# Causal attention block: the maximum's mask moved from TensorE matmuls to VectorE, and the shift rows from TensorE and ScalarE to VectorE and DRAM

## What is computed

```python
def reference(x, w_in, w_out, W_r, W_k, W_v, mu_r, mu_k):   # x: 2 x 2048 x 256
    xn = layernorm(x)
    q, k, v = heads(xn @ w_in.T)                  # 16 heads of 16
    att = q @ k.T / 4
    att = where(tril, att, 0.0)                   # masked scores are 0, not minus infinity
    a = softmax(att) @ v
    r = sigmoid((mu_r*xn + (1-mu_r)*x_prev) @ W_r.T)
    kk = square(relu((mu_k*xn + (1-mu_k)*x_prev) @ W_k.T))
    return x + merge(a) @ w_out.T + r * (kk @ W_v.T)
```

## Time and profile before

| | us |
|---|---|
| median of 3 runs | 1128.43 |
| lowest, highest | 1125.78, 1129.91 |
| the profiled execution | 1134.35 |
| its span | 1132.6 |
| TensorE busy in the span | 1080.0 (95%) |
| VectorE busy | 842.5 (74%) |
| ScalarE busy | 713.4 (63%) |
| GpSimd busy | 385.8 (34%) |

### The profile page before, as it was taken

How to read it: one execution, slowest core, us unless ns; L and a number is a source line. 1 busy time by engine, 2 the same in 40 slices (tenths; PEclk the granted TensorE clock), 3 DMA queues, 4 the chain that set the end, 5 groups by cost and what they waited for, 6 DMA issues and landing times.

```text
span 1132.6 us, 21906 instructions
## 1 busy us (share of the span) xinstructions
PE 1080.0 (95%) x8192; PEld 542.6 (48%) x8192; DVE 842.5 (74%) x1153; ACT 713.4 (63%) x1519; POOL 385.8 (34%) x945
## 2 busy tenths in 40 slices
PE   5999998999999999999989999999999989999998
PEld 3665554544444444444435444444444434444445
DVE  5567787678879787987867878878887878789213
ACT  2433333267776677777757776777777657767672
POOL 3211121354414341444224424442532433244301
PEclk9999999999999899999969999999999989999999
DMA  3585744392019000900280019002800460002033
GB/s 127 174 271 177 214 149 149 131 117 62 2 20 122 30 3 17 124 31 7 37 119 11 6 22 140 8 7 38 124 6 6 58 104 7 6 2 86 25 98 117
DMA packets 53390, 83.61 MB, mean 74 GB/s; under 512 B 6308, under 2 KB 36260, under 8 KB 49572
## 3 DMA queue, kind: packets, MB, share of 16 engines
q1 hardware_dynamic: 52132, 78.01, 32.9%
q0 software_dynamic: 1152, 4.19, 1.2%
HBM read 43.78 MB, written 33.55 MB: 68 GB/s over the span
## 4 chain that ended last, share of the span: by engine, by line
PE 75%; DVE 13%; ACT 4%; issue 4%; DMA 2%; POOL 0%; SPq 0%; ACTq 0%; DVEq 0%; POOLq 0%
PE ps_o L1189 22%; PE ps_s L1175 21%; DVE part_max L347 10%; PE ps_m L330 7%; PE ps_vr L733 4%; ACT probs L1039 4%; PE ps_qk L724 4%; PE ps_m L1220 3%; PE ps_o L1200 2%; PE ps_m L337 2%; PE ps_xt L782 2%; PE ps_qk L733 2%; PE ps_s L1164 2%; DMA x_in<-x 1%; PE ps_pieces L330 1%
## 5 line engine op out<-in xcount | busy, mean ns | idle before, releaser
L1039 ACT ACTIVATE probs<-ps_s 128x512 f32<-128x512 f32 (+3 forms) x1280 | 599.6, 536 | 249.6 <-PE ps_s L1175 241.5
L347 DVE TENSOR_REDUCE part_max<-ps_m 128x2 f32<-128x1024 f32 (+2 forms) x594 | 616.6, 1059 | 152.7 <-PE ps_m L330 115.1
L1175 PE MATMUL ps_s<-q_op,k_op 50*128 50x512 f32 (+3 forms) x1280 | 447.9, 429 | 10.0 <-ACT probs L1039 5.2
L330 PE MATMUL ps_m<-k_op,q_op 48*128 48x512 f32 (+3 forms) x1188 | 355.3, 419 | 16.6 <-DVE part_max L347 9.4
L1175 PEld LDWEIGHTS ps_s<-q_op,k_op 50*128 50x128 f32 x1280 | 210.7, 188 | 313.1 <-ACT probs L1039 214.2
L984 POOL TENSOR_SCALAR_AFFINE_SELECT probs<-probs 128x128 f32<-128x128 f32 x512 | 145.0, 292 | 485.7 <-ACT probs L1039 477.2
L1189 PE MATMUL ps_o<-probs,v_sb 128*32 128x512 f32 (+3 forms) x2560 | 307.9, 551 | 2.2 <-issue 2.2
L330 PEld LDWEIGHTS ps_m<-k_op,q_op 48*128 48x128 f32 x1188 | 169.3, 189 | 43.8 <-DVE part_max L347 33.8
L950 POOL TENSOR_TENSOR diag_weight<-ident,masked_weight 128x256 f32<-128x256 f32 x256 | 150.5, 623 | 40.7 <-ACT masked_weight L1005 40.7
L337 PE MATMUL ps_m<-mask,pick 64*128 64x64 bf16 (+1 forms) x932 | 96.5, 210 | 0.0
L1189 PEld LDWEIGHTS ps_o<-probs,v_sb 128*32 128x32 f32 x2560 | 51.1, 108 | 76.7 <-issue 38.1
(11 more groups left out here) (81 smaller groups left out, 715.9 us busy)
## 6 DMA issues: line engine op xcount, KB each, us to landing
parts_d<-parts SPq DMA_DIRECT2D x32, 512.0 KB, 4.7
q_op<-parts_d SPq DMA_DIRECT2D x42, 256.0 KB, 13.9
k_op<-parts_d SPq DMA_DIRECT2D x42, 256.0 KB, 16.2
vpad_d<-v_pad SPq DMA_DIRECT2D x32, 256.0 KB, 3.3
v_sb<-vpad_d SPq DMA_DIRECT2D x8, 1024.0 KB, 12.4
x_in<-x SPq DMA_DIRECT2D x8, 512.0 KB, 5.2
ffn_d<-ffn SPq DMA_DIRECT2D x8, 512.0 KB, 3.2
attn_t<-normed SPq DMA_DIRECT2D x128, 32.0 KB, 2.0
```

Of the source, the lines that this page charges most:

```text
L330: last = pe.matmul(ps_m[:, f % ring * 2 + e, 0:width], self.q_op[rows, p, j, q0:q0 + P], self.k_op[rows, p, j, pc * CH:pc * CH + width], s ...
L347: dve.tensor_reduce(both, ps_m[:, bank:bank + 2, 0:width], AX_X, ALU.max).then_inc(self.piece_reduced, 1)
L1039: act.activation(probs[:, slot % PRING, 0:width], ps_s[:, bank_of("scores", slot, first, last), 0:width], ACT.Exp).then_inc(probs_ready, 1)
L1175: pe.matmul(ps_s[:, bank_of("scores", slot, first, last), 0:CH - q0], k_op[rows, p, h % 2, kt * P:(kt + 1) * P], q_op[rows, p, h % 2, u * ...
```

## The change

**TensorE** no longer adds the mask: the four L337 matmuls of each diagonal piece are gone (1024 in all), and so are the 32 turns of shift rows, four transposes each. **ScalarE** no longer copies them. The ring of `ps_s` banks has one use less for each.

**VectorE** reduces a diagonal piece in parts: the blocks left of the diagonal block as before, with one reduction (none where there is no such block), and the diagonal block of each head with one `tensor_tensor_reduce`, which adds the fp32 `mask` and takes the maximum in one pass, writes the sum back to PSUM and the maximum to `part_max`. It is built as two instructions, the pass and one that writes the maximum out. A fourth `max_step` transposes the 32 columns of `shift` in blocks of 32 x 32 into `shift_t`.

**SyncE** gets the shift rows from `shift_t` into `q_op` in two hops: four DMAs to a DRAM buffer `shift_d`, a wait until they have landed, four DMAs to `q_op`. And in `group`, the loads of the next group's queries and keys now stand behind `keep_normed` of the previous group's unit 3 and behind `place_shift` of unit 2.

```diff
@@ -211,12 +210,12 @@
         self.v_after = sb("v_after", [P, 2, NT, GH * HW])
         self.keys_after = sb("keys_after", [P, P])
         self.ones = sb("ones", [P, P])
-        self.mask16 = sb("mask16", [P, 2, P], BF16)
-        self.pick16 = sb("pick16", [P, 2, P], BF16)
+        self.mask = sb("mask", [P, P])
         self.part_max = sb("part_max", [P, NCH, GH * SUB, NCH + 1])
+        self.floor = sb("floor", [P, 2])
         self.row_max = sb("row_max", [P, NCH, GH, SUB])
         self.shift = sb("shift", [P, NCH, SUB, SHIFT_PARTS, GH])
-        self.shift_t = sb("shift_t", [SHIFT_PARTS * GH, 2, CH])
+        self.shift_t = sb("shift_t", [P, 2, HW])
 
         self.consts_set, self.consts_made = sem("consts_set"), sem("consts_made")
         self.q_loaded = [sem("q_loaded0"), sem("q_loaded1")]
...
@@ -229,36 +228,28 @@
         self.after_ready = sem("after_ready")
         self.ones_placed = sem("ones_placed")
         self.chunk_loaded = [sem(f"chunk_loaded{c}") for c in range(NCH)]
-        self.shift_turned, self.shift_t_ready = sem("shift_turned"), sem("shift_t_ready")
+        self.shift_t_ready, self.shift_stored = sem("shift_t_ready"), sem("shift_stored")
         self.shift_loaded = [sem("shift_loaded0"), sem("shift_loaded1")]
         self.SHIFTS = SHIFT_PARTS * 2 * 16
+        self.shift_d = nc.dram_tensor("shift_d", [2, SHIFT_PARTS, 2, GH // 2, CH], F32, kind="Internal").ap()
         self.parts_in = parts_d.rearrange("r (z b) (cc g e j d) t -> r z (b cc) g e d j t", b=B, cc=CC, g=2, e=2, j=GH // 2)
...
-        pool.memset(self.pick16[:], 0.0).then_inc(self.consts_set, 1)
+        pool.memset(self.mask[:], 0.0).then_inc(self.consts_set, 1)
+        pool.memset(self.floor[:], 0.0).then_inc(self.consts_set, 1)
         pool.memset(self.part_max[:], 0.0).then_inc(self.consts_set, 1)
         pool.memset(self.after[:, NT - 1], 0.0).then_inc(self.consts_set, 1)
         pool.wait_ge(self.consts_set, 5)
...
-                pool.wait_ge(self.consts_made, 1 + 4 * e + 2 * half)
-                mask, pick = self.mask16[rows, half], self.pick16[rows, half]
-                pool.affine_select(out=mask, in_=mask, compare_op=ALU.is_ge, fill=NEG, base=half * HALF,
-                                   pattern=[[-1, P]], channel_multiplier=1).then_inc(self.consts_made, 1)
-                pool.wait_ge(self.consts_made, 2 + 4 * e + 2 * half)
-                pool.affine_select(out=pick, in_=pick, compare_op=ALU.not_equal, fill=1.0, base=half * HALF,
-                                   pattern=[[-1, P]], channel_multiplier=1).then_inc(self.consts_made, 1)
-        pool.wait_ge(self.consts_made, 9)
-        floor = self.part_max[:, NCH - 1].rearrange("p (h s) c -> p h s c", s=SUB)[:, :, SUB - 1, NCH]
-        pool.affine_select(out=floor, in_=floor, compare_op=ALU.not_equal, fill=LOWEST,
-                           base=-(P - 1), pattern=[[0, GH]], channel_multiplier=1).then_inc(self.consts_made, 1)
+        pool.affine_select(out=self.mask[:], in_=self.mask[:], compare_op=ALU.is_ge, fill=NEG, base=0,
+                           pattern=[[-1, P]], channel_multiplier=1).then_inc(self.consts_made, 1)
+        pool.wait_ge(self.consts_made, 2)
+        pool.affine_select(out=self.floor[:], in_=self.floor[:], compare_op=ALU.not_equal, fill=LOWEST,
+                           base=-(P - 1), pattern=[[0, 2]], channel_multiplier=1).then_inc(self.consts_made, 1)
 
         for half in range(2):
             counts = self.v_after[:, half].rearrange("p t (h w) -> p t h w", w=HW)[:, :, :, HD:HW]
@@ -300,11 +291,16 @@
     def place_shift(self, sp, p, u, n):
 
         sp.wait_ge(self.shift_t_ready, n + 1)
+        sp.wait_ge(self.shift_loaded[u % 2], (n // 2 + 1) * self.SHIFTS)
+        by_block = self.shift_d[u % 2].rearrange("r e j (s b w) -> b s (r e j) w", s=SUB, w=HW)
+        for b in range(P // HW):
+            sp.dma_start(by_block[b], self.shift_t[b * HW:(b + 1) * HW, u % 2]).then_inc(self.shift_stored, 16)
+        sp.wait_ge(self.shift_stored, (n + 1) * (P // HW) * 16)
         for part in range(SHIFT_PARTS):
             for e in range(2):
-                row, at = e * HALF + ROWS + part, part * GH + e * 2
+                row = e * HALF + ROWS + part
                 sp.dma_start(self.q_op[row:row + 1, p, :, u * CH:(u + 1) * CH].bitcast(F32),
-                             self.shift_t[at:at + 2, u % 2]).then_inc(self.shift_loaded[u % 2], 16)
+                             self.shift_d[u % 2, part, e].unsqueeze(0)).then_inc(self.shift_loaded[u % 2], 16)
 
     def load_values(self, sp, i, p):
 
@@ -328,14 +324,7 @@
         for e in (1, 0):
             rows = slice(e * HALF, e * HALF + ROWS)
             last = pe.matmul(ps_m[:, f % ring * 2 + e, 0:width], self.q_op[rows, p, j, q0:q0 + P],
-                             self.k_op[rows, p, j, pc * CH:pc * CH + width], start=True, stop=(pc < u))
-        if pc == u:
-
-            for k in range(2):
-                for e in (1, 0):
-                    half = slice(e * HALF, (e + 1) * HALF)
-                    last = pe.matmul(ps_m[:, f % ring * 2 + e, s * P + k * HALF:width], self.pick16[half, k],
-                                     self.mask16[half, k, k * HALF:P], start=False, stop=(k == 1))
+                             self.k_op[rows, p, j, pc * CH:pc * CH + width], start=True, stop=True)
         last.then_inc(self.piece_ready, 1)
 
     def reduce_piece(self, dve, ps_m, ring, f, base):
@@ -343,8 +332,17 @@
         u, j, s, pc, width = piece(f)
         dve.wait_ge(self.piece_ready, base + f + 1)
         bank = f % ring * 2
-        both = self.part_max[:, u].rearrange("p (e j s) c -> p e j s c", j=GH // 2, s=SUB)[:, :, j, s, pc]
-        dve.tensor_reduce(both, ps_m[:, bank:bank + 2, 0:width], AX_X, ALU.max).then_inc(self.piece_reduced, 1)
+        by_pair = self.part_max[:, u].rearrange("p (e j s) c -> p e j s c", j=GH // 2, s=SUB)[:, :, j, s]
+        if pc < u:
+            dve.tensor_reduce(by_pair[:, :, pc], ps_m[:, bank:bank + 2, 0:width], AX_X, ALU.max).then_inc(self.piece_reduced, 1)
+            return
+        if s > 0:
+            dve.tensor_reduce(by_pair[:, :, pc], ps_m[:, bank:bank + 2, 0:s * P], AX_X, ALU.max)
+        for e in range(2):
+            block = ps_m[:, bank + e, s * P:width]
+            floor = self.floor[:, 0:1] if u == NCH - 1 and s == SUB - 1 else 0.0
+            last = dve.tensor_tensor_reduce(block, block, self.mask[:], 1.0, floor, ALU.add, ALU.max, by_pair[:, e, pc + 1:pc + 2])
+        last.then_inc(self.piece_reduced, 1)
 
     def max_step(self, dve, k, u, n, reduced):
 
@@ -361,6 +359,11 @@
             dve.wait_ge(self.hi_ready, n + 1)
             dve.scalar_tensor_tensor(by_head[1], self.row_max[:, u], -1.0, by_head[0], ALU.mult,
                                      ALU.subtract).then_inc(self.shift_ready, 1)
+        if k == 3:
+            dve.wait_ge(self.shift_ready, n + 1)
+            if n >= 2:
+                dve.wait_ge(self.shift_stored, (n - 1) * (P // HW) * 16)
+            dve.transpose(self.shift_t[:, u % 2], self.shift[:, u].rearrange("p s r h -> p (s r h)")).then_inc(self.shift_t_ready, 1)
 
     def after_piece(self, dve, f, n0, base, close):
 
...
@@ -889,16 +867,14 @@
                 sp.dma_start(out_tiles[n], total[n % ORING]).then_inc(out_stored[n % ORING], 16)
 
             def group(i, p, first=False, last=False):
-                if not last:
-
-                    if not first:
-                        sp.wait_ge(scores_ready, (i * 2 + p) * SLOTS)
-                    ops.load_scores(sp, i + p, 1 - p)
                 if not first:
                     keep_normed(i - 1 + p, 1 - p, NCH - 1)
                 ops.place_shift(sp, p, 2, unit_of(i, p, 2))
                 if not last:
 
+                    if not first:
+                        sp.wait_ge(scores_ready, (i * 2 + p) * SLOTS)
+                    ops.load_scores(sp, i + p, 1 - p)
                     sp.wait_ge(masked_done, unit_of(i, p, 0) + 1)
                     sp.wait_ge(probs_used, weighed_to(unit_of(i, p, 0)))
                     ops.load_values(sp, i + p, 1 - p)
...
-                    v = SHIFT_AT[u, kt]
-                    wait_for_bank("shift", v, i, p, first, last)
-                    turn_shift(v, unit_of(i, p, v + nxt), bank_of("shift", v, first, last))
+                    sum_suffix(1 - p, SV_AT[u, kt], G + 1, bank_of("suffix", SV_AT[u, kt], i * 2 + p))
 
             def group(i, p, first=False, last=False):
                 G = i * 2 + p
```

78 lines of the change are left out of this document (18 added, 60 removed).

## The result

The changed kernel takes **1181.6 us** (median of four runs, 1170.2 to 1199.9) where the kernel before takes 1129.2 beside it. The longest of the four counts as a slow run; without it the median is 1177.8 and the ratio 1.043, 95% interval 1.034 to 1.052. The kernel is slower, as forecast, and some 23 us less slow than forecast. The profiled execution is that longest one, 1199.9 us with a span of 1198.0.

A forecast was written before the change was run, and what follows sets the result against it. The prediction took a loop of TensorE and ScalarE waiting for each other, 2.67 us a key tile, as the bound, VectorE second. Terms 0 - 16 + 11 + 73.5 + 18 - 10 = +76.5 gave 1205 us against the median; range 1165 to 1240.

The forecast's parts named there:

- masks and passes: Diagonal pieces: mask matmuls off TensorE gain 0, being hidden; VectorE's added passes cost +11 us, +1.5 a group.
- turns of shift rows: Turns off TensorE and ScalarE: 32 tiles with a turn each become 0.5 us shorter, -16 us.
- losses of before: Waits for "issue" and low-clock slices near group starts, 19 us together; half taken as gone, -10 us.
- stops for late loads: Piece 0 of the next group waits for queries and keys: 12 us in six groups, 1.5 in the first.
- clock behind them: After each 12 us stop, some 9 us of work at the lower clock: 3 us, six times, +18.
- the choice inside the bounds: Wait of piece 0 for late loads, bounded at 9.8 to 15.7 us; 12 was taken.
- The row of the prediction for the price: Fourth group's 98 matmuls at half clock, 20.5 us against 13.4: 0.35 us lost per microsecond at the lower level.
- the rival with 20 us behind each stop: Clock stays low for 20 us after each stop: +7 six times in place of +3, 1229 us; chance 0.12.
- The rival of the full price: On VectorE, pass and second instruction do not overlap: +38 in place of +11, 1232 us; chance 0.10.
- the rival of TensorE as the bound: Mask matmuls count on TensorE, 0.26 us off each of 256 pieces: 1127 us with loads still late; chance 0.03.
- One rule for all tiles from rows 3: Key tiles last 2.67 us with or without mask matmuls, so masks cost nothing; at most 1 us a group.
- the hop "costs nothing": Shift rows' way through DRAM, some 4 us longer, is covered by many key tiles before a unit's first score.

The follow-up runs named there:

- 1096.2: Kernel before with shift rows through VectorE and DRAM, masks still on TensorE, SyncE issuing shift rows, then loads, then results: 1096.2 us, ratio 0.967.
- 1093.6: Changed kernel with SyncE issuing shift rows, then loads, then results, plus 128 met waits at the start of TensorE's program: 1093.6 us, ratio 0.966.
- 1108.6: Kernel before with only the masks moved to VectorE, plus 128 met waits at the start of TensorE's program: 1108.6 us, ratio 0.979.
- 1132.1: Kernel before, unchanged, timed beside one of the three sets of experiment kernels: 1132.1 us.
- 1094.1: Changed kernel with SyncE issuing unit 2's shift rows first, then query and key loads, then the previous group's results: 1094.1 us, ratio 0.966.

## Why the prediction was right, and what of it was wrong

The side, the deciding term and its place were right; the size was too high by 23 us. Its sum by parts, with what the runs show in place of each (differences of medians; the stops from the profiled execution):

| term | forecast | measured | from |
|---|---|---|---|
| masks and passes | 0 + 11 | -2.6 | 1096.2 (masks on TensorE) to 1093.6, within the noise |
| turns of shift rows | -16 | -15.0 | 1108.6 to 1093.6, no gap in either |
| losses of before | -10 | -20.8 | 1132.1 to 1096.2, less the turns |
| stops for late loads | +73.5 | +56.0 | the row of the waits |
| clock behind them | +18 | +31.5 | what is left: 1181.6 less 1094.1 less 56.0 |
| sum | +76.5 | +49.1 | |

Three terms were too high, the loads by 17.5 us, masks and passes by 13.6 and the losses of before by 10.8, and the clock's was too low by 13.5. The clock's row is a remainder, so the sum has to come out near the measured difference (1.043 is 49 us) and proves nothing; the rows for themselves count.

**Loads.** The working held to a microsecond: first load 23.9 us into the group forecast (475.0 less 451.1), 23.6 measured (the stores landed in 1.1 us, not in the 2.0 of a result); from first issue to last landing 30.2 to 36, measured 30.6; a stop of 9.8 to 15.7, measured 9.3 in the mean. The step that failed is the choice inside the bounds. I took 12 "nearer to the case that a row shows", to leave room for values that share the engines. They hardly do: the run with the values held back gained 0.9 us. The low end was the right one, 56 us in place of 72. The first group, for which I gave 1.5, had no stop.

**Clock.** Here the term was too small. I took 9 us at the lower level behind each stop. In the profiled execution each of the six stretches begins within its stop, which costs nothing yet, and goes on behind it, from the matmul of piece 0, for 31.5, 7.5, 33.2, 15.7, 41.8 and 4.6 us, 22 in the mean; a seventh, of 13.7 us in the last group, follows no stop. The row of the prediction for the price was good: in the second group nearly the same work, from piece 0 on, takes 30.8 us in the change and 20.7 us with the loads in time:

```profile
383.70:414.50 30.80, 30.80 (x139) 13.54 (x143) 18.14 (x67) 14.84 (x34) 13.95 (x39) 0.50 0.08 27
```

```profile
372.84:393.50 20.66, 19.31 (x140) 8.12 (x140) 18.75 (x72) 14.43 (x34) 12.47 (x37) 1.00 0.12 38
```

10.1 us lost in 30.8, 0.33 us per microsecond at 1.2 GHz, where I had 0.35. The Trainium skill (TensorE: Matmul & The Clock Gate, Terms) puts the penalty at half of the throttled time; by that estimate this stretch would cost 15.4 us. This kernel pays less; the likely reason, which no run tests, is that at the higher clock TensorE and ScalarE wait for each other in part of the time. What failed is the length, and it is not one length: behind stops at the same place of the same code it goes from 4.6 to 41.8 us in one execution, and from 7.4 to 34.2 with the values held back. I can't say what ends a stretch. It goes with the spread of the four runs: 1170.2, 1177.8, 1185.4 and 1199.9 us had a mean granted clock of 0.952, 0.940, 0.936 and 0.921, that is 112, 141, 152 and 189 us at the lower level. If what lay in the stops and in the last group was the same in all four (55 us in the profiled one), some 10 to 16 us stood behind each stop in the three shorter runs; that is an estimate. So the rival with 20 us behind each stop describes the profiled execution, and the others lie between it and my 9.

**VectorE.** Forecast for a pass with its second instruction, the readout, 0.30 us. The timeline of VectorE in the change, and in the kernel with only the masks moved the reduction behind a second pass:

```profile
522.98 0.29 DVE L344 CUSTOM_DVE_ANT_0 ps_m<-ps_m,mask 128x128 f32<-128x128 f32 x1
523.19 0.14 DVE L344 DVE_READ_ACCUMULATOR2_ANT part_max<- 128x1 f32 x1
523.19 0.33 DVE L344 CUSTOM_DVE_ANT_0 ps_m<-ps_m,mask 128x128 f32<-128x128 f32 x1
523.44 0.14 DVE L344 DVE_READ_ACCUMULATOR2_ANT part_max<- 128x1 f32 x1
```

```profile
600.05 0.32 DVE L339 CUSTOM_DVE_ANT_0 ps_m<-ps_m,mask 128x128 f32<-128x128 f32 x1
600.30 0.13 DVE L339 DVE_READ_ACCUMULATOR2_ANT part_max<- 128x1 f32 x1
600.30 0.69 DVE L335 TENSOR_REDUCE part_max<-ps_m 128x2 f32<-128x512 f32 x1
```

From the start of a pass to the start of what follows it are 0.21 us (the second pass) and 0.25 (the reduction): each readout starts together with the next instruction, and 0.04 is the most that it can be seen to cost here. The busy time of a group grows by 6.4 us, 0.20 a piece in place of 0.31, and VectorE's by 52 us in place of 80. Of that 0.8 us a group reach the end in the order of before (1.5 forecast), and nothing in the last one. The rival of the full price, which needed over 0.4 us for a pass with its readout, is out. The Trainium skill (VectorE: DVE Perf Modes, the section on the TRN2 errata) has 120 + N cycles for an instruction from PSUM to SBUF, by my estimate 0.26 us for this pass, which goes from PSUM to PSUM; the trace has the next instruction 0.21 to 0.25 us after it, and 0.31 us as the mean length of its record.

**Masks: 0.** The tile of 2.67 us stayed 2.67, so the rival of TensorE as the bound is out in such tiles. But in tiles that hold output matmuls too, masks count: key tiles 4, 7 and 9 of a unit of 16 took 3.57, 3.46 and 3.51 us before and 3.40, 3.27 and 3.33 without masks. One rule for all tiles from rows 3 was the mistake, worth 1.26 us a group, a little over the bound I had kept. Those three tiles hold 0.54 of it, the rest is spread over short tiles.

**Turns: -16.** Right; -15.0 measured, and the tile with a turn goes from the 3.18 us of rows 4 to 2.66 in the change. The gain appears only if the hop is in time. The sentence that the hop "costs nothing" held in the change and fails with loads first: five waits in the kernel with only the shift rows changed, 3.2 us in the mean and 4.3 at most, and the lower clock behind them.

**Losses of before.** The step that failed most in proportion. Stops and clock were priced at 19, measured at 20.8, but I took half as gone for no other reason than that their place moves. In the change all are gone: no gap for "issue" over 0.8 us in attention but the six. The four gaps of before stood 17 us into a group (575.8, 910.2) or 27 (365.4, 703.1). In the change the loads don't run yet at 17 us, but they do at 27, and with the loads from 13.4 us on they run at both, in three kernels; no gap came. Why one place of the code meets a gap and another doesn't is open.

## What to carry to other kernels

Write down for every load when it is first issued, how long the whole batch takes, and when its first reader is due: here the sum of the three gave each stop within half a microsecond, and moving four small DMAs a group on one queue was worth 87 us. A small store that something waits for belongs ahead of a batch of large loads, and what nobody waits for behind it. A difference of a per cent or two between two kernels is no price of the edit while idle gaps and the lower clock move with the place of the code: compare undisturbed groups, or shift the code by idle instructions and time again.

## What the runs showed of the hardware

- 128 met waits at the start of TensorE's program made one kernel 11 us faster (0.991) and another 5 us, with gaps of 1 to 3 us moved or gone. All 15 such gaps in the traces end 3.2 to 3.8 us after a 16 KB packet of instructions started.
- Here transfers behaved as if served in the order of issue: 1 MB issued right behind 3 MB of loads delayed the last of them by 0.9 us, while four stores of 4 KB issued behind the loads took 10.8 us after their last issue in place of 1.1.
- Stops of 9 us were followed by anything from 4.6 to 41.8 us at the granted clock of 0.50, at the same place of the same program; in the four kernels without a gap over 1 us in attention the clock stayed at 1.00 there up to the last 3 us; in the one without masks it fell once for 10.2 us with no such gap before.
- The accumulator's readout of a `tensor_tensor_reduce` (141 ns) runs beside the next instruction, which starts 0.21 to 0.25 us after the pass over 128 elements.
